# Third layer of a graph network: one product of 512 columns for the edge attributes of four tiles

## The reference, cut to what matters

```
m_input  = concatenate([node_states[src], node_states[dst], edge_rel_emb])   # 128 + 128 + 64 wide
h        = relu(m_input @ W1 + b1)
messages = relu(h @ W2 + b2)
agg      = segment_sum(messages, dst)
updated  = node_states + relu(agg @ Wn + bn)
return layer_norm(updated, gamma, beta)
```

## Time and profile before

| | |
|---|---|
| median of 3 runs | 5880.88 us |
| the profiled execution, its own time | 5894.55 us |
| its span, first to last instruction | 5892.8 us |
| mean granted TensorE clock | 0.804 |
| busy: PE / weight loads / DVE / ACT / POOL | 3522.7 / 2842.9 / 2457.4 / 861.6 / 3258.2 us |
| matmuls / weight loads | 18892 / 18893 |

### The profile page before, as it was taken

The page is one execution under the profiler, slowest core; times in us unless marked ns, Lnnn a source line. Parts: engine busy times, 40 slices in busy tenths (PEclk is TensorE's granted clock), DMA queues, the critical chain, the costliest instruction groups (busy, mean ns, idle before and its releaser), DMA issues.

```text
span 5892.8 us, 77533 instructions
## 1 busy us (share of the span) xinstructions
PE 3522.7 (60%) x18892; PEld 2842.9 (48%) x18893; DVE 2457.4 (42%) x5306; ACT 861.6 (15%) x2555; POOL 3258.2 (55%) x3346
## 2 busy tenths in 40 slices
PE   3555555564777777667327777777775344445555
PEld 2333333343555555555226667666674233333333
DVE  5445444552444444444413434333347122222237
ACT  0000000031222222222101111111114000000005
POOL 6666666635555555553565555555541666666651
PEclk9999999976888888888558888888897555555567
DMA  3141111124555555554134444444441111111112
GB/s 89 45 136 44 45 45 44 43 82 106 134 137 136 136 137 134 135 137 120 49 90 111 109 108 110 108 107 108 111 111 56 46 45 46 44 43 46 44 41 62
DMA packets 600706, 512.64 MB, mean 87 GB/s; under 512 B 99918, under 2 KB 532221, under 8 KB 600590
## 3 DMA queue, kind: packets, MB, share of 16 engines
q0 software_dynamic: 105728, 217.12, 14.5%
q10 hardware_dynamic: 204320, 151.42, 9.6%
q1 hardware_dynamic: 290542, 142.84, 8.9%
HBM read 411.48 MB, written 91.26 MB: 85 GB/s over the span
## 4 chain that ended last, share of the span: by engine, by line
another core or an unknown queue 40%; issue 16%; PE 12%; DVEq 10%; DVE 8%; ACTq 6%; ACT 4%; POOL 1%; DMA 1%; SPq 0%; POOLq 0%
PE bank L639 12%; DVEq L1398 3%; DVEq L1380 2%; ACT acc L992 2%; ACTq L1015 2%; DVEq L336 2%; ACTq L996 1%; ACTq L1018 1%; ACTq L1021 1%; DVE acc L1382 1%; PE bank L644 1%; DVE quads L1390 1%; DVE work L1411 1%; DVE bst L1427 0%
## 5 line engine op out<-in xcount | busy, mean ns | idle before, releaser
L1382 DVE TENSOR_TENSOR acc<-bank,acc 128x512 f32 x588 | 406.8, 692 | 1388.0 <-remote 1023.9
L639 PE MATMUL bank<-quads,work 128*128 128x128 f32 x3920 | 834.0, 318 | 139.4 <-issue 138.6
L639 PEld LDWEIGHTS bank<-quads,work 128*128 128x128 f32 x3920 | 713.6, 234 | 182.2 <-issue 181.9
L537 POOL DMA_INDIRECT g<-a_src,srcq x392 | 380.7, 971 | 339.2 <-ACT srcq L1004 232.5
L537 POOL DMA_INDIRECT nodes<-xl,srcq x392 | 378.8, 966 | 339.3 <-ACT srcq L1004 232.6
L639 PE MATMUL bank<-quads,g 128*128 128x128 f32 x1568 | 399.6, 412 | 263.2 <-issue 215.5
L537 POOL DMA_INDIRECT g<-xl,srcq x392 | 380.1, 970 | 306.5 <-ACT srcq L1004 188.0
L537 POOL DMA_INDIRECT nodes<-a_src,srcq x392 | 378.9, 966 | 298.3 <-ACT srcq L1004 171.2
L537 POOL DMA_INDIRECT g<-x,srcq x392 | 370.5, 945 | 235.0 <-issue 116.8
L639 PEld LDWEIGHTS bank<-quads,g 128*128 128x128 f32 x1568 | 330.8, 299 | 351.2 <-issue 351.0
L537 POOL DMA_INDIRECT work<-x,srcq x392 | 377.9, 964 | 218.9 <-issue 116.9
(11 more groups left out here) (338 smaller groups left out, 6272.4 us busy)
## 6 DMA issues: line engine op xcount, KB each, us to landing
partial<-acc ACTq DMA_DIRECT2D x196, 288.0 KB
work<-local_rank ACTq DMA_DIRECT2D x392, 128.0 KB
work<-xr_by_rank SPq DMA_DIRECT2D x784, 64.0 KB
work<-b_by_rank SPq DMA_DIRECT2D x784, 64.0 KB
work<-in_rel_t ACTq DMA_DIRECT2D x196, 128.0 KB
g<-acc SPq DMA_DIRECT2D x126, 64.0 KB, 1.8
g<-in_x,srcq POOLq DMA_INDIRECT x392
nodes<-in_x,srcq POOLq DMA_INDIRECT x392
```

The costliest lines, as they stand in the source:

```text
L537: pool.indirect_dma_start(quad_rows(l, q)[:, t, :], None, table, bass.IndirectOffsetOnAxis(srcq[:, s * TQ + t:s * TQ + t + 1].bitcast(U32) ...
L639: return nc.tensor.matmul(to, lhsT, rhs, start=start, stop=stop, skip_group_check=True)
L1382: v.tensor_tensor(window, partial_bank(l, q)[:, :], window, ALU.add).then_inc(partial_copied, 1)
```

## The change

In `expand_mlp` the four tiles are turned first, one behind the other. Then one product of `w1c` with all 512 columns of the quad's edge attributes is added to the whole bank, and then the four window products follow. A `start` flag on a product or a turn makes what it writes replace what the bank held. Only the first turned tile has the flag now; before, each had it.

```
-            def flip(to, src, stop=True):
+            def flip(to, src, start=True, stop=True):
 
                 k = src.shape[0]
-                return nc.tensor.matmul(to, src, ident[0:k, 0:k], start=True, stop=stop, is_transpose=True,
+                return nc.tensor.matmul(to, src, ident[0:k, 0:k], start=start, stop=stop, is_transpose=True,
                                         skip_group_check=True)
...
                 for t in range(TQ):
-                    to = bank[r][:, t * P:(t + 1) * P]
-                    flip(to, quad_rows(2, q)[:, t, :], stop=False)
-                    mm(to, w1c[:], rel[:, s, t * P:(t + 1) * P], start=False, stop=False)
-                    last = mm(to, win[:, s * TQ + t, :], onehot_t[:, r, t * P:(t + 1) * P], start=False)
+                    flip(bank[r][:, t * P:(t + 1) * P], quad_rows(2, q)[:, t, :], start=t == 0, stop=False)
+                mm(bank[r][:, :], w1c[:], rel[:, s, :], start=False, stop=False)
+                for t in range(TQ):
+                    last = mm(bank[r][:, t * P:(t + 1) * P], win[:, s * TQ + t, :], onehot_t[:, r, t * P:(t + 1) * P],
+                              start=False)
                 last.then_inc(expanded[2], 1)
```

## The result

The changed kernel takes 5855.58 us (median of 10 runs, 5849.38 to 5863.07), the kernel before 5881.76 us (10 runs on the same chip, 5872.54 to 5901.99). The ratio is 0.9951, 95% interval 0.994 to 0.9962: 0.5% faster, some 26 us, and beyond the 0.2% that I called no change. The time lies in the range, but the likeliest case, no change, did not come true, and the favourable shift that had 0.08 did.

What follows compares the result with a forecast made beforehand. It took the third layer to be bound by late releases of `hidden` behind GpSimd's gathers, not by matmuls. 5894.6 - 0.4 = 5894.2 us profiled, less 13.7 over the median, gave 5880.5, stated as 5880; range 5765 to 5905.

Steps and rivals of the forecast that it cites:

- the likeliest case: Whole kernel: 5880 us, no change (difference below 0.2%, some 12 us), reaching from 5869 to 5892; chance 0.57.
- the favourable shift: Third layer's quads: releases of `hidden` shift among their steps by chance, shortening the kernel by 12 us or more; chance 0.08.
- backlog rival: TensorE's own backlog delays `hidden`; six loads fewer save 0.67 us in each of 196 quads, 131 us: 5750; chance 0.22.
- Columns: `w1c` product in `expand_mlp`: two 512-column passes take 0.88 us at full clock, 1.70 at the lower; difference 0.00 to -0.01.
- Weight loads: Six of eight `w1c` loads per quad go, counted at nothing; row -0.01 us, ends -1.31 and +0.44.
- The product isn't split: `w1c` group: 392 matmuls and 392 loads in all; a compiler split into 128-column passes would still give 5880 us.
- Order and the single start flag: `expand_mlp`: turned tiles wait for the same gathers, the last window product still raises the semaphore, the flag issues nothing.
- The release of `hidden` is held by GpSimd's gathers: Third layer: TensorE's semaphore updates can be held during gathers, coming about 1 to 2 us behind them.
- On the path: A shorter expansion counts only where TensorE ended `hidden`'s wait, 37 of 180 quads; scaled, 40 x -0.01 = -0.4 us.
- a sum near 940 us of remote: Sign that the forecast is right: `hidden` still waits mostly for "remote", near 940 us in the same stretch.

Runs made afterwards that it cites:

- e7: The kernel before with one GpSimd gather of four per quad in the third layer, other tiles keeping old rows: ratio 0.9131 to the kernel before.
- e4: The changed kernel with one GpSimd gather of four per quad in the third layer, other tiles keeping old rows: ratio 0.9104 to the kernel before.
- e1: The changed kernel with its new order and single start flag, but four w1c products of 128 columns instead of one of 512: ratio 0.9999 to the kernel before.
- e12: The changed kernel with two gathers of four per quad in the third layer, other two tiles keeping old rows: ratio 0.9123 to the kernel before.
- e8: The changed kernel with one gather of four; the other three tiles come as SyncE's plain DMAs of fixed rows: ratio 0.9112 to the kernel before.
- e5: The changed kernel with one gather of four, plus twelve GpSimd scratch-tile writes, each followed by a drain: ratio 1.0466 to the kernel before.
- e2: The changed kernel plus three one-column w1c products per quad (six matmuls, six loads) into an unused bank: ratio 1.0031 to the kernel before.
- e6: The changed kernel with two w1c products of 256 columns instead of one of 512: ratio 0.9987 to the kernel before.
- e10: The changed kernel with the second layer's four 128-column products also made one of 512, leaving messages transposed: ratio 0.9937 to the kernel before.

## Why the prediction was right and wrong

*The range: right by its width.* It reached 115 us below the forecast to take in most of the backlog rival, which did not come true as priced. That 5855.58 lies in it is in good part luck and says little for the working; the forecast itself, 5880 and no change within 12 us, missed by 24.

*Columns: right.* I gave 0.88 us to two passes of 512 columns at full clock and 1.70 at the lower one. The next group starts 0.86 us after the product at full clock (3436.91 to 3437.77), and 1.71 at the lower: the changed kernel's timeline has the product at 4007.49 and its successor at 4009.20. The expansion from first start to last end is 2.35 us, 2.39 in the earlier trace rows.

*Weight loads: right.* I took -0.01 us a quad between -1.31 and +0.44. With every quad on the path the whole change is -0.035 us (e7 against e4), where six steps not covered would be -0.67. "TensorE: Matmul & The Clock Gate" of the Trainium skill, section "The mechanism", lists as overlapping only loads on other row groups than the matmuls in flight; the measurement, a twentieth of six steps, speaks against that. The text of the same section also lets a load for the background weight buffer go ahead, which the prediction passed over; the measurement doesn't contradict that, and no run here shows which buffer a load goes to.

*The product isn't split: right.* 378 matmuls of 512 columns for 189 quads.

*Order and the single start flag, nothing: right*, e1.

*The release of `hidden` is held by GpSimd's gathers: right*, and no longer an inference from two places. One gather instead of four removes it (e4, e7), as do two that are over before the expansion ends (e12). As many bytes by SyncE don't bring it back (e8), nor do GpSimd's writes (e5).

*Backlog, the rival with 0.22 (the prediction once calls it the second; it is the third of its list): wrong as priced.* If instructions or loads ran behind their records, `hidden` would stay late with one gather in the kernel before, which has all eight matmuls and loads of `w1c`. It does not: median 0.04 us (e7). And leaving the product out entirely gives 0.6%, not the 2.2% that I priced for six loads. Beside running gathers, though, the number of instructions does seem to matter; see what stays open.

*The step that failed is the sum "On the path".* It read: only where TensorE ended the wait, 37 of 180 quads, does a shorter expansion end earlier, so 40 x -0.01 us; and against the favourable shift it said that "the expansion's end moves by 0.01 us, and 196 quads average out". They do not average out, because quads are not independent. A prompt release lets the indices be copied before GpSimd has finished a series, two series join, and two quads share one late release. The loop of 7.5 us and the pair of 13.5 are two courses of one and the same program. The set of prompt quads was not a constant of the kernel, as I took it, but something that the change moves: 37 of 180 became 113 of 189, while the layer became 23.5 us shorter. That the first brings the second is the reading that fits these two traces; e2 and e6, with about as many prompt quads and little or no gain, show that the count alone doesn't give it. The forecast sign "a sum near 940 us of remote" failed with it, at 566.3.

*What stays open* is why one long product tips more quads into pairs. It is not the order (e1). It has no fixed price per instruction: by what stands on `w1c`, with the columns alike, the ratios are 0.9999 for 8 + 8 (e1), 0.9987 for 4 + 4 and 0.9951 for 2 + 2, and 6 + 6 fewer elsewhere bring 0.14% more (e10), within the intervals.

The traces do say that the recorded moment alone doesn't decide. Take the quads whose expansion ended 4.0 to 4.3 us behind the `hidden` before, as it does at full clock in a quad like that of the earlier trace rows, and count those released within 0.5 us:

| expansion ended behind the `hidden` before | before | e1 | e6 | change | e10 |
|---|---|---|---|---|---|
| 4.0 to 4.3 us | 5 of 100 | 11 of 104 | 17 of 65 | 25 of 42 | 26 of 30 |
| 5.6 to 6.0 us | 6 of 39 | 2 of 28 | 23 of 26 | 13 of 14 | 8 of 8 |

The second row has quads with stretches at the lower clock, which end when the fourth gather has been started. Their commonest end is the same, 5.76 us, before, in e1 and with the change, where in the first row it is 4.12, 4.12 and 4.09. In both the prompt share goes with the number of loads and matmuls on TensorE: as many as before in e1, four pairs fewer in e6, six in the change, twelve in e10. So what an update finds in its way seems to depend on how many instructions TensorE has behind it, and not only on the gathers. That would be a small form of the backlog rival that shows only beside gathers. It is read off single traces, whose expansion ends are modelled, and is not shown by an experiment: no run moves the update by a chosen amount and nothing else.

## What to carry to other kernels

Before a matmul edit is priced, ask of the wait behind it whether it follows the matmul's end at all, quad by quad; where it is released late by a second loop, here GpSimd's gathers, shortening the matmuls is worth next to nothing in itself. But don't forecast "no change" from that alone: in such a loop a small shift can turn single late quads into pairs, so look for the second course of the loop in the trace, price it per quad, and give it a real chance. The lever is the loop itself: fewer gathers in a series, or their trigger placed ahead of other work, as the copy of the indices ahead of `hidden`, which alone brought the kernel before to 0.9944.

## What the runs showed of the hardware

A series of four indirect gathers on GpSimd, 0.95 us each and 1.25 us from start to start, holds back the semaphore updates of TensorE that VectorE, ScalarE and SyncE wait for. Without it, and without the time of three of the gathers themselves, the kernel takes 0.9104 of the time before; the hold's part is at most some 7% by the estimate in e4. An update that comes within a series of the loop is seen up to 5.4 us late in the traces of the kernel before and of the change (3443.31 to 3447.92, 4.6 us, in the stretch shown). The longer the series, the longer the hold: as the layer starts, GpSimd runs gathers one after the other until 3060.78, and the update at the end of this expansion, 3023.66, reaches ScalarE after 47 us:

```profile
3022.08 1.58 PE L639 MATMUL bank<-quads,work 128*128 128x128 f32 x8
...
3059.84 0.94 POOL L537 DMA_INDIRECT g<-a_src,srcq  x1 [0.30 <-issue]
...
3070.86 0.69 ACT L1158 ACTIVATE quads<-bank,b1c 128x512 f32<-128x512 f32 x1 [58.87 <-remote]
```

Some 10 us of this lie behind the last of these gathers, which I can't explain. With one gather a quad the same update is 0.04 us late (e4). One that comes when the series is already through is seen 0.04 to 0.12 us later in the median (e4, e12). But an update may also pass in the midst of a series, as at 3438.93 above, and I can't say by what rule. Plain DMAs, with the traffic at 177 GB/s, and writes on GpSimd don't hold updates (e8, e5).

Without the hold TensorE ran 700.00 of 700.00 us at a granted clock of 1.00, where it had 0.85 to 0.89 with gaps: the stretches at the lower clock went away with the late releases.

Products of one column are not cheap beside others: six more matmuls and six more loads of this kind took 0.59 us (e2), 0.1 us for each pair of load and matmul, almost what a pair with 128 columns takes (0.111). So a short product is bounded by something other than its columns. Upwards the time goes by the columns: 0.43 us for a pair with 512 is four times 0.108. The long product saves next to nothing on TensorE because 128 columns already take as long as such a pair needs at least (0.035 us a quad, e7 against e4).
